# A four-pass graph network on one core: the row of numbers that one-hots are compared with moves from SBUF to a PSUM bank

## What is computed

```python
# block 0: three graph layers with edge features (this change touches it)
for l in range(3):
    e = edge_attr_64 @ We[l] + be[l]
    m = relu(h[src] + e)
    agg = segment_sum(m, dst)
    h = layer_norm(relu(relu((h + agg) @ W1[l] + b1[l]) @ W2[l] + b2[l])) * gamma + beta
# block 1: attention per relation (5 relations), softmax over each node's edges, elu
# block 2: typed attention, 8 heads: first pass scores and their maxima per node, second pass sums
#          (this change touches the first pass)
scores = (Q[dst] * K_edge_type[src]).sum(-1) / 4 * mu
smax   = segment_max(scores, dst);  ex = exp(scores - smax[dst]);  agg = segment_sum(V[src] * w)
# block 3: message passing on [x[src], x[dst], edge_attr_32], layernorm
```

## Time and profile before

| | |
|---|---|
| median of three runs | 4971.89 us |
| the profiled execution | 4978.06 us |
| its span in the profile | 4976.0 us |
| PE, DVE, ACT, POOL busy | 3122, 2700, 722, 2928 us |
| mean granted TensorE clock | 0.734 of full |
| POOL's indirect DMAs | 400 scatters, then 6 passes of 416 gathers |

### The profile page before, as it was taken

The page is one execution under the profiler, slowest core; times in us unless marked ns, Lnnn a source line. Parts: engine busy times, 40 slices in busy tenths (PEclk is TensorE's granted clock), DMA queues, the critical chain, the costliest instruction groups (busy, mean ns, idle before and its releaser), DMA issues.

```text
span 4976.0 us, 85301 instructions
## 1 busy us (share of the span) xinstructions
PE 3122.3 (63%) x20716; PEld 2741.5 (55%) x20717; DVE 2700.0 (54%) x8043; ACT 721.8 (15%) x1742; POOL 2927.5 (59%) x2911
## 2 busy tenths in 40 slices
PE   0000098886777767776664557767777788667776
PEld 0000088885666656666454346545555688566665
DVE  5100088885444444444667955546666566655553
ACT  1000022222111111111110034420000000411111
POOL 3767677774777747777057877037777000067772
PEclk9999999997555555555765589875555699888886
DMA  6333255554222232223276279476656444033332
GB/s 218 75 89 77 74 154 148 156 153 88 79 76 76 74 61 76 76 75 76 71 208 175 85 199 227 118 206 173 171 171 170 96 126 126 5 91 92 91 92 45
DMA packets 643811, 577.27 MB, mean 116 GB/s; under 512 B 235163, under 2 KB 535800, under 8 KB 643576
## 3 DMA queue, kind: packets, MB, share of 16 engines
q0 software_dynamic: 99328, 211.51, 18.2%
q1 hardware_dynamic: 389624, 235.01, 16.3%
q10 hardware_dynamic: 154752, 129.55, 9.4%
HBM read 424.35 MB, written 151.40 MB: 116 GB/s over the span
## 4 chain that ended last, share of the span: by engine, by line
POOL 50%; issue 20%; PE 14%; DMA 8%; DVE 5%; ACT 1%; SPq 1%; DVEq 0%; POOLq 0%; ACTq 0%
POOL ring L811 29%; POOL HA L829 8%; POOL arena L838 8%; POOL slot_records L797 5%; PE ps L2282 3%; PE ps L2131 2%; DMA ring<-table_gine,idx 2%; DMA arena<-in_edge_attr 2%; DMA table_rel<-arena 1%; PE ps L2283 1%; PE ps L2149 1%; PE ps L2245 1%; DMA slot_records<-arena,slotr 1%; PE ps L1950 1%; DVE HA L854 1%
## 5 line engine op out<-in xcount | busy, mean ns | idle before, releaser
L811 POOL DMA_INDIRECT ring<-table_gine,idx x1248 | 1249.6, 1001 | 498.3 <-issue 370.2
L811 POOL DMA_INDIRECT ring<-table_msg,idx x416 | 398.3, 958 | 630.3 <-DMA table_msg<-arena 503.7
L854 DVE TENSOR_TENSOR mraw<-ps,ring 128x512 f32<-128x512 f32 x416 | 287.7, 691 | 779.4 <-DMA ring<-table_gine,idx 344.1
L838 POOL DMA_INDIRECT arena<-table_keys_values,idx x416 | 435.2, 1046 | 335.8 <-DVEq L186 207.3
L1993 PE MATMUL ps<-oh,msg 128*128 128x128 f32 x1664 | 423.4, 435 | 317.6 <-DVE HA L854 222.8
L829 POOL DMA_INDIRECT HA<-table_rel,idx x416 | 447.1, 1075 | 292.0 <-DMA table_rel<-arena 165.4
L1993 PEld LDWEIGHTS ps<-oh,msg 128*128 128x128 f32 x1664 | 364.5, 323 | 376.2 <-DVE HA L854 345.2
L854 DVE TENSOR_TENSOR HA<-HA,ps 128x128 f32 (+1 forms) x1664 | 476.3, 286 | 165.7 <-DVE HA L854 146.3
L1960 PE MATMUL ps<-wt,ear 65*128 65x128 f32 x2496 | 518.4, 378 | 16.0 <-DMA ear<-edge_attr_T 15.8
L797 POOL DMA_INDIRECT slot_records<-arena,slotr x400 | 392.8, 982 | 213.7 <-issue 123.2
L1960 PEld LDWEIGHTS ps<-wt,ear 65*128 65x128 f32 x2496 | 491.5, 292 | 16.9 <-issue 16.3
(11 more groups left out here) (379 smaller groups left out, 5911.3 us busy)
## 6 DMA issues: line engine op xcount, KB each, us to landing
ear<-edge_attr_T SPq DMA_DIRECT2D x312, 128.0 KB
ear<-slot_rows ACTq DMA_DIRECT2D x312, 128.0 KB
oh<-slot_rows ACTq DMA_DIRECT2D x104, 256.0 KB
slot_values<-HA SPq DMA_DIRECT2D x104, 256.0 KB
ring<-slot_values ACTq DMA_DIRECT2D x104, 256.0 KB
slot_values<-arena SPq DMA_DIRECT2D x104, 256.0 KB
ring<-slot_values SPq DMA_DIRECT2D x104, 256.0 KB, 3.0
slot_records<-msg SPq DMA_DIRECT2D x32, 650.0 KB, 11.6
```

The lines of the kernel that those rows point to most:

```text
L811: pool.indirect_dma_start(out=ring[:, k % 4, j, 0:width], out_offset=None, in_=table[:, :], in_offset=bass.IndirectOffsetOnAxis(ap=idx[:, ...
L838: pool.indirect_dma_start(out=kvring[:, k % 4, j, :], out_offset=None, in_=tab2[:, :], in_offset=bass.IndirectOffsetOnAxis(ap=idx5[:, k * ...
L854: return V.tensor_tensor(o, x, y, op)
```

## The change

`iota_ps`, 128 columns of bank 1 of PSUM, gets a copy of `iota_n` at the start of each graph layer and before the first typed pass. Three comparisons read the numbers there: the one-hot of the graph layers, the permutation `perm` of the sort, and `end_onehots` of the first typed pass. The other one-hots (relation pass, second typed pass, message pass) still read `iota_n` in SBUF. To free bank 1, edge terms of layer 0 use bank 0 alone, where each batch waits until the one before has been added; those of layers 1 and 2 alternate between banks 0 and 2 (they had four); the turned maxima use bank 0 alone, with a wait until ACT has taken the ones before. DVE's wait for `pn_free` in layers 1 and 2 stands ahead of the copy now, where it stood ahead of the loop.

```diff
+        iota_ps = ps[:, 1, 0:P]
...
-                tt(buf[:, t.s4 % depth], iota_n[:, :].unsqueeze(1).to_broadcast([P, B, P]),
+                numbers = iota_ps if made is qg["onehot"] else iota_n[:, :]
+                tt(buf[:, t.s4 % depth], numbers.unsqueeze(1).to_broadcast([P, B, P]),
                    dl[:, bass.ds(t.k * B, B)].unsqueeze(2).to_broadcast([P, B, P]), ALU.is_equal).then_inc(made, 1)
...
-                tt(perm[:, t.h], iota_n[:, :].unsqueeze(1).to_broadcast([P, B, P]),
+                tt(perm[:, t.h], iota_ps.unsqueeze(1).to_broadcast([P, B, P]),
...
-                tt(mraw[:, t.h], ps[:, t.s4 if t.of else t.h, :].rearrange("p (j d) -> p j d", j=B), ring[:, t.s4, :, 0:D], ALU.add).then_inc(qg["added"], 1)
+                tt(mraw[:, t.h], ps[:, 2 * t.h if t.of else 0, :].rearrange("p (j d) -> p j d", j=B), ring[:, t.s4, :, 0:D], ALU.add).then_inc(qg["added"], 1)
...
+                if l:
+                    dve.wait_ge(pn_free, xt_done[l - 1] + GRP)
+                ch(V.tensor_copy(iota_ps, iota_n[:, :]))
...
-                    dve.wait_ge(pn_free, xt_done[l - 1] + GRP)
...
-                tt(oh[:, t.s4], iota_n[:, :].unsqueeze(1).to_broadcast([P, B, P]),
+                tt(oh[:, t.s4], iota_ps.unsqueeze(1).to_broadcast([P, B, P]),
...
+            ch(V.tensor_copy(iota_ps, iota_n[:, :]))
             ch_tr = Steps(dve, trs_sem, 3)
...
-                A.activation(gm[:, t.s4, :, 0:NHEAD], ps[:, t.h, 0:B * NHEAD].rearrange("p (j g) -> p j g", j=B), ACT.Copy).then_inc(qm["picked"], 1)
+                A.activation(gm[:, t.s4, :, 0:NHEAD], ps[:, 0, 0:B * NHEAD].rearrange("p (j g) -> p j g", j=B), ACT.Copy).then_inc(qm["picked"], 1)
...
-                if t.of or t.late(2):
-                    pe.wait_ge(qg["added"], t.n - (3 if t.of else 1))
+                if t.of or t.late(1):
+                    pe.wait_ge(qg["added"], t.n - (1 if t.of else 0))
...
-                    ins = M.matmul(ps[:, t.s4 if t.of else t.h, j * P:(j + 1) * P], ear[0:EA + 1, t.h, j * P:(j + 1) * P],
+                    ins = M.matmul(ps[:, 2 * t.h if t.of else 0, j * P:(j + 1) * P], ear[0:EA + 1, t.h, j * P:(j + 1) * P],
...
-                if t.late(2):
-                    pe.wait_ge(qm["picked"], t.n - 1)
+                if t.late(1):
+                    pe.wait_ge(qm["picked"], t.n)
...
-                M.transpose(ps[:, t.h, 0:B * NHEAD], sf[:, t.h, :], ident[0:B * NHEAD, 0:B * NHEAD]).then_inc(qm["back"], 1)
+                M.transpose(ps[:, 0, 0:B * NHEAD], sf[:, t.h, :], ident[0:B * NHEAD, 0:B * NHEAD]).then_inc(qm["back"], 1)
```

## The result

The change takes **4890.2 us** (median of five; 4886.0 to 4915.6) where the kernel before takes 4971.9 (five runs, 4960.0 to 4988.5). The ratio is 0.984, with a 95% interval of 0.981 to 0.987: faster, by 1.6%. The forecast was 4868, so 82 us of the 104 came. The experiments add a reservation: on another chip, where the kernel before already takes 6091 us, the same change is slower, by 0.7%.

A forecast was written before the change was run, and what follows sets the result against it. POOL's gathers were taken to set the pace in the graph layers and first typed pass. Removed delays -107.9, `ohT` +3 and copies +1 gave -104 us, from 4971.9 to 4868 us, range 4850 to 4900.

The forecast's parts named there:

- What bounds the kernel: Graph layers and first typed pass: POOL's 416 gathers per stage set the length, 520 us if none is held.
- Removed delays, 107.9 us: Gathers held by DVE's two-SBUF comparisons: 25.3, 20.7 and 21.5 us in layers 0 to 2, 40.4 in the typed pass.
- Comparisons at the same cost: DVE's comparisons with numbers in PSUM keep their 684 ns.
- `ohT` left over, 3 us: Typed pass: the unchanged `ohT` still holds some gathers, +3 us, between nothing and 23.
- Copies, 1 us: Four 128x128 copies of the numbers into PSUM, 0 to 1 us, taken as 1.
- Edge terms in one bank, 0: Layer 0: PE's edge terms wait for DVE's last addition, price 0, bounds 0 and all of the layer's 25 us.
- laid-out turn: Layer 0: one turn's new chain, `moved` over at about +4.2 us, within DVE's 4.43 and POOL's 5.0.
- slower* rival: Layer 0: the bank wait puts gaps into PE's turns, the clock falls to half, +244 us there, 5133 total; chance 0.04.
- What becomes late next in the typed pass, 0 us (bound 10): Typed pass: gathers wait for scores of four batches before; 1.7 us reserve remain, 0 us, up to 10 if `rz` is late.
- rival *nothing changes: Gathers stay held by something PSUM does not remove, such as the second input; 4972 within a few us; chance 0.03.

The follow-up runs named there:

- f1_layer0_sbuf: The change with layer 0's one-hot and permutation reading numbers from SBUF again, its edge terms still in one bank: 4921.3 us, ratio 0.990.
- f2_change_third: The change itself, run again unchanged beside the kernel before: 4890.1 us, ratio 0.984.
- f4_resets_again: The change with the typed pass's `rz` rows fetched one batch earlier by SP: 4882.0 us, ratio 0.983.
- third set: Four follow-up kernels run together with the kernel before, which took 4970.0 us there, on a chip like that of the result.
- f3_order_again: The kernel before, numbers in SBUF, with the one-hot of layers 1 and 2 after two of DVE's four additions: 4940.4 us, ratio 0.994.
- second set: Follow-up kernels run on a slower chip, where the kernel before took 6091.2 us and the unchanged change 6131.5 us, ratio 1.007.

## Why the prediction was right, and by how much it was off

The forecast, faster, and its range held; the point lay 22 us too low. Step by step:

- **What bounds the kernel.** Right, for the chip of the result: each of the three graph layers shrank by what POOL's busy time fell; the typed pass shrank by 25 us of 40.
- **Removed delays, 107.9 us.** Right. Layer 0 lost 26.8 us, layer 1 21.5 and layer 2 23.1 (forecast 25.3, 20.7, 21.5), POOL's busy time in the typed pass 40.0 (40.4). That the PSUM source does it is shown by `f1_layer0_sbuf` for layer 0, and what is held by the starts: all 49 gathers over 1.0 us of layer 1 began during a one-hot (the prediction says all but two), and 47 starts during `arena<-ps,small` (it says 44) were not held. In the typed pass the same is read from the profile after; no run on such a chip took that part back alone. Behind it stands the Trainium skill's inference (SBUF — State Buffer, Who interferes with whom) that a `tensor_tensor` should not delay a gather's descriptors: `f1_layer0_sbuf` contradicts it: 19.2 us of held time in layer 0, and none in `f2_change_third` on the same chip, with nothing changed but DVE's source.
- **Comparisons at the same cost.** Right, 684 ns.
- **`ohT` left over, 3 us.** Right: 1.7 us of held time in the stage, on 15 gathers, 11 of them beside `ohT`. **Copies, 1 us**: nothing to be seen; the pieces between the layers are 52.8 and 46.6 us long, before 52.6 and 47.9.
- **Edge terms in one bank, 0.** Right. The laid-out turn had the edge terms at +1.43 and `moved` over at +4.2; the trace has +1.44 and +4.26. DVE waited 5.1 us for `moved` in the whole layer. The fall of the clock that the *slower* rival had did not come; the layer's mean rose from 0.91 to 0.98.
- **What becomes late next in the typed pass, 0 us (bound 10).** This term was mis-sized. The working gave the scores 8.6 us from the end of a batch's gathers, read off one turn, and so 1.7 us of reserve. Over all turns the median was 8.8 before and is 10.0 after. SP's issue of a batch's values, which waits for the landing, comes 2.7 us after its gathers' end, where it was 1.9 (why the landing is later is not shown), `rz` is issued behind it, and the scan starts 4.0 us after that issue (3.7). The reserve fell from 2.25 to 0.8 us at the median, and 38 of POOL's gathers waited. Measured: 17 us of such waiting, 15 more than before, over the bound of 10. `f4_resets_again` shows that it was `rz`: fetched a batch earlier it gives 18 us back in the stage.
- **Left out of the sum.** The forecast took everything between the stages as fixed. It is not. The piece between the relation and the typed pass is 6 us longer in the profile after, and 10 to 12 in the four of the third set, `f3_order_again` too, which has no number in PSUM; PE had 909 matmuls left there before, and 920 to 960 after. What decides how many are left was not tried, and with one profile of the kernel before it is not shown that the change has a part in it. And the second typed pass has a spread of its own, below. Added up from the profile before to that of `f2_change_third` (4976.0 to 4886.1 us): the four stages -93, the piece before the typed pass +10, the second typed pass -8, all else +2.

For the chip of the second set the forecast would have been wrong in sign: 0.7% slower. The rival *nothing changes* comes nearest there, but not for its reason: the gathers did become short, and nobody waited for them.

## What to carry to other kernels

When a gather is sometimes long, look at what stands on DVE at its start. An operation on two SBUF tiles held it here until that operation's end; putting one source in PSUM cured that at no cost for DVE, and so does moving the operation to a place between two starts where DVE's turn is tied to the gathers, which needs no bank. Before counting on a faster engine, take the reserve of the next chain as a distribution over all turns and not from one; here 1.7 us by one turn was 0.8 at the median once POOL ran faster. And a gain in the pace of one engine is worth something only where that engine is waited for: this change gained 1.6% where the kernel before takes 4970 us and lost 0.7% where it takes 6091, so run such a pair on more than one chip.

## What was not expected of the hardware

- **Chips differ.** The same kernel takes 4970 us on one and 6091 and 6138 on two others, with the same durations of gathers (medians of 0.944 and 0.947 us) and comparisons (684 ns). There an addition starts 15.5 us after its batch's last gather at the median of layer 1 instead of 1.8, mostly only after POOL has paused for 2 to 3 us. Why is open.
- **The second typed pass depends on when the clock rises.** The clock is at half level (0.50) through the typed pass and rises some time after, to fall again only for 50 us in all in the last 125 of the pass. (Five of the six profiles also have it up for 3.4 us some 45 us in, which is left aside here.) In the profile before it rose 69 us after the last typed gather, in the profile after 165 us, with PE busy 145 of these 165 us:

```profile
3869.60:3938.90 69.30, 49.23 (x269) 44.70 (x269) 35.05 (x124) 4.08 (x14) 0.01 (x1) 0.50 0.34 77
3869.60:4373.40 503.80, 403.38 (x3642) 371.69 (x3642) 321.38 (x873) 82.74 (x237) 0.06 (x2) 0.88 0.33 89
```
```profile
3775.00:3940.10 165.10, 145.41 (x848) 140.86 (x849) 75.33 (x224) 8.66 (x34) 0.02 (x1) 0.51 0.31 80
3775.00:4313.10 538.10, 445.72 (x3642) 415.77 (x3642) 323.19 (x873) 82.70 (x237) 0.04 (x2) 0.80 0.30 83
```

The second typed pass is 503.8 us long in the one and 538.1 in the other. The other four profiles at this speed fall in line: rise after 53.8, 79.0, 91.7 and 157.3 us, length 495.4, 506.8, 512.8 and 534.9 (`f2_change_third`, `f1_layer0_sbuf`, `f4_resets_again`, `f3_order_again`). That is 0.38 us more per microsecond of later rise, up to 43 us between executions, more than some of the effects that the study was after. The profiled execution of the change (4915.6 us) is 25 us over its median, and this is most likely why: `f2_change_third`, the same kernel, has 495.4 us there and 4888.2 in all. What decides when the clock rises is not shown by these runs.
